# Routed experts, latent attention and the feed-forward's end: another order of the steps on four engines

## The reference

```python
x = x + grouped_attention(layernorm(x), ctx, ctx)            # 32 query heads, 8 key heads
x = x + routed_ffn(layernorm(x), ...)                        # 8 experts + 4 "zero" ones, best 2
x = x + latent_attention(layernorm(x), ctx, Wq, w_kc_q, ...) # 16 heads, rotary, latent of 192 and 64
x = x + mx_ffn(layernorm(x), w_gate, w_up, w_down)           # block-quantised feed-forward
# routed_ffn: w[b,s,e] = 1.5 * prob for the best two of 12
#   out = sum_e w_e * down_e(silu(gate_e(y)) * up_e(y)) + y * sum of the weights of the zero experts
# mx_ffn: inputs and weights in blocks of 32 with a shared power of two, elements rounded and clipped
```

## Time and profile before

| | us |
|---|---|
| median of 3 runs | 820.71 (819.5 to 823.96) |
| profiled execution, its own time | 820.66 |
| its span, first to last instruction | 818.8 |
| PE busy in the span | 751.6 (92%) |
| DVE busy | 597.1 (73%) |
| POOL busy | 567.7 (69%) |
| ACT busy | 404.4 (49%) |

### The profile page before, as it was taken

One profiled execution on the slowest core, in us unless ns is written; L12 is line 12 of the kernel. 1 busy time (PEld: TensorE's weight loads), 2 busy tenths in 40 slices (PEclk: granted clock), 3 DMA queues, 4 the chain that ended last, 5 costly groups with the idle time before them and its releaser, 6 DMA issues. The chain is left out here.

```text
span 818.8 us, 14824 instructions
## 1 busy us (share of the span) xinstructions
PE 751.6 (92%) x4808; PEld 539.1 (66%) x4808; DVE 597.1 (73%) x1087; ACT 404.4 (49%) x1068; POOL 567.7 (69%) x590
## 2 busy tenths in 40 slices
PE   4999999878999998889999999999999999876786
PEld 2555455457888887756777777777777777663454
DVE  5899999866777878666465575886678676739995
ACT  1688888532323323226455545545454545444463
POOL 5667766434867667365666878787878787817996
PEclk9999999999999999899999999999999999987999
DMA  9200000040100010321200000000000000000001
GB/s 252 119 1 0 0 0 1 1 171 1 39 20 19 19 58 0 107 82 63 87 12 1 1 1 2 2 1 1 1 1 2 2 1 1 1 2 7 26 29 44
DMA packets 8764, 24.12 MB, mean 29 GB/s; under 512 B 1712, under 2 KB 5168, under 8 KB 8088
## 3 DMA queue, kind: packets, MB, share of 16 engines
q1 hardware_dynamic: 8154, 23.28, 8.6%
q10 hardware_dynamic: 549, 0.08, 0.1%
HBM read 21.26 MB, written 2.10 MB: 29 GB/s over the span
## 5 line engine op out<-in xcount | busy, mean ns | idle before, releaser
L1620 POOL TENSOR_TENSOR q<-turned 64x512 f32<-64x512 f32 x128 | 167.9, 1312 | 25.5 <-DVE turned L1546 9.9
L1297 PE MATMUL ps<-l_yt,a 128*128 128x512 f32 x576 | 145.5, 403 | 2.1 <-ACT p L1443 1.6
L1297 PEld LDWEIGHTS ps<-l_yt,a 128*128 128x128 f32 x576 | 105.8, 190 | 27.7 <-issue 4.7
L1607 POOL TENSOR_TENSOR p<-p,l_inverse 128x512 f32<-128x512 f32 x64 | 66.9, 1047 | 76.4 <-DVE l_inverse L1568 75.9
L1443 ACT ACTIVATE p<-ps,l_negmax 128x128 f32<-128x128 f32 x256 | 91.0, 382 | 43.2 <-DVE l_negmax L1537 43.1
L1546 DVE TENSOR_TENSOR turned<-ps,rope 128x1024 f32<-128x1024 f32 x64 | 78.1, 1221 | 44.4 <-PE ps L1297 41.7
L879 PE MATMUL ps<-yt_experts,wsplit 128*128 (+1 forms) x384 | 97.2, 402 | 0.2 <-DVE inner L977 0.2
L467 DVE TENSOR_REDUCE negmax<-ps 128x4 f32<-128x512 f32 x128 | 84.3, 685 | 12.8 <-PE ps L290 12.2
L879 PEld LDWEIGHTS ps<-yt_experts,wsplit 128*128 128x128 f32 x384 | 71.2, 192 | 14.4 <-DVE inner L977 0.5
L1537 DVE TENSOR_REDUCE l_negmax<-ps 128x4 f32<-128x512 f32 x64 | 41.2, 686 | 45.9 <-PE ps L1355 45.7
L383 ACT ACTIVATE pt<-ps 128x512 f32<-128x512 f32 x128 | 70.9, 599 | 6.1 <-PE ps L312 3.8
(11 more groups left out here) (214 smaller groups left out, 1549.6 us busy)
## 6 DMA issues: line engine op xcount, KB each, us to landing
wide<-in_wide SPq DMA_DIRECT2D x8, 768.0 KB, 4.3
mx_raw<-in_mx SPq DMA_DIRECT2D x8, 384.0 KB, 3.1
x<-in_x SPq DMA_DIRECT2D x4, 512.0 KB, 8.7
ctx_t<-in_ctx_t SPq DMA_DIRECT2D x1, 2048.0 KB, 8.5
out<-x SPq DMA_DIRECT2D x16, 128.0 KB, 1.7
narrow<-in_narrow SPq DMA_DIRECT2D x8, 192.0 KB, 2.6
ktraw<-in_ctx_rows SPq DMA_DIRECT2D x1, 1248.0 KB
wraw<-in_gate SPq DMA_DIRECT2D x1, 1024.0 KB, 18.6
```

The source lines that it names most:

```text
L1297: out = pe.matmul(tile_bank(n, k), a[i][:, pa, kin, k * 128:(k + 1) * 128], yt[j % 2][:, py, kin, :, :].rearrange("p b s -> p (b s)"), sta ...
L1607: pool.tensor_tensor(p[:, head, :, :], p[:, head, :, :], spread(inverse[:, head, :], 2, S), ALU.mult).then_inc(normed[head], 1)
L1620: t = pool.tensor_tensor(out[rows[(head + half) % 2], head, :], turned[rows[head], half, :], turned[rows[head], 2 + half, :], ALU.add)
```

## The change

Experts: on DVE the five instructions of `shift` are cut in two, `shift_up` (three) and `shift_down` (two). In odd steps `hidden` stands between them (in group 0 ahead of the quantising in every step). On POOL x is scaled in x = 5 and 6 instead of 6 and 7, and `ht` of unit 0 is made one step earlier. The last units are written out by hand on each engine (`last`), with a second PSUM bank for the last weights and the last chunk's transposes. The constant `lowest` is set as a 22nd step of the routes.

Latent attention: PE's order is `tile` (3), `narrow_product`, `context` of n-3, `score` of n-1, `turn_p` (both), `project` of n-3 (both); the 128-column matmul of `narrow_product` becomes two of 64 columns. PSUM banks are handed out anew (`ctx_ps`, `turned_p_bank`) with waits that fit; the places of `spare` are handed out anew; the front's parts on DVE move from the end of the step to behind the maxima, some a step later. Feed-forward: scaling back of sequence 14 and of the second half of sequence 15 moves from POOL to DVE.

```diff
@@ experts, PE: the end written out
+                pe.wait_ge(h_made, UNITS - 2)
+                spread_weights(UNITS - 2, weight_ps)
+                pe.wait_ge(gated_made, UNITS - 1)
+                spread_weights(UNITS - 1, last_weight_ps)
+                down(UNITS - 3)
+                pe.wait_ge(inner_made, UNITS - 1)
+                turn_tiles(CHUNKS - 2)
+                down(UNITS - 2)
+                down(UNITS - 1)
+                pe.wait_ge(mx_kept, CHUNKS - 1)
+                turn_tiles(CHUNKS - 1)
@@ experts, DVE step
-                if first and u == 2:
+                early = first and u < EXPERTS
+                if inside(u - 2, UNITS) and early:
                     hidden(u, par)
                 if inside(v, UNITS):
-                    (shift if x % 2 else block_powers)(v, jv, xv)
+                    if x % 2:
+                        shift_up(v, jv, xv)
+                    else:
+                        block_powers(v, jv, xv)
...
-                if inside(u - 2, UNITS) and not (first and u == 2):
+                if inside(u - 2, UNITS) and not early:
                     hidden(u, par)
+                if inside(v, UNITS) and x % 2:
+                    shift_down(v, jv, xv)
@@ experts, POOL step
-                if inside(u, UNITS) and x == 7:
+                if inside(u, UNITS) and x == 6:
                     pool.wait_ge(affine, j + 4)
+                if first and u == 2:
+                    low_part(0, 0)
+                if inside(u - 3, UNITS) and not (first and u == 3):
+                    low_part(u - 3, old)
                 if inside(v, UNITS):
+                    quantise(4 * jv + xv // 2, xv)
                 if inside(u, UNITS) and x < ROTARY_STEPS:
                     rotate_context(pool, m, rotated, j, x)
-                if inside(u, UNITS) and x in (6, 7):
+                if inside(u, UNITS) and x in (5, 6):
                     scale_x(j, x)
@@ latent attention, PE
-                    pe.matmul(q_ps, b[i][:, 1, :], q[n % 2][:, 2, :], start=False, stop=True).then_inc(narrowed, 1)
+                    for head in range(2):
+                        t = pe.matmul(q_ps[rows[head], :], b[i][:, 1, head * CE:(head + 1) * CE], q[n % 2][:, 2, :],
+                                      start=False, stop=True)
+                    t.then_inc(narrowed, 1)
...
                 narrow_product(n - 1)
                 spare(n, 1)
+                context(n - 3)
+                score(n - 1)
                 turn_p(n - 2, 0)
+                turn_p(n - 2, 1)
+                spare(n, 2)
                 project(n - 3, 0)
-                turn_p(n - 2, 1)
                 project(n - 3, 1)
-                spare(n, 2)
-                score(n - 1)
-                context(n - 2)
                 spare(n, 3)
@@ latent attention, DVE
                 maximum(n - 2, 1)
+                for k, part in ((3, f.add), (4, f.statistics), (6, f.scales), (7, f.divide), (8, f.clip), (9, f.multiply)):
+                    if front_in(n, k) is not None:
+                        part(dve, m, front_in(n, k))
                 rotate_both(n, 0)
...
-                for k, part in ((2, f.add), (3, f.statistics), (6, f.scales), (7, f.divide), (8, f.clip), (8, f.multiply)):
-                    if front_in(n, k) is not None:
-                        part(dve, m, front_in(n, k))
@@ feed-forward, DVE at n == B
                 if n == B:
+                    scale_back(n - 2)
                     clip_halves()
+                    scale_back_half()
```

More of the change, by code:

```diff
@@ L821, in routed_experts, with steps @@
         weights_turned_ps = weight_ps[0:WROWS, :]
-        def steps(engine, step):
+        def steps(engine, step, last):
             def group(j):
@@ L831, in steps @@
                 group(j)
-            for x in range(3):
-                step(UNITS + x, GROUPS, x)
+            last()
         @block.sync
@@ L919, in _, with last, spread_weights, down @@
             t.then_inc(logits_turned, 1)
-            steps(pe, step)
+            def last():
+                def spread_weights(u, bank):
+                    pe.matmul(bank, select[:, u % EXPERTS, :], weights_t[:, GROUPS - 1, :],
+                              start=True, stop=True).then_inc(weight_spread, 1)
+                def down(u):
+                    expert = u % EXPERTS
+                    pe.wait_ge(h_lo, u + 1)
+                    for q, (ph, pw) in enumerate(PRODUCTS):
+                        for s in range(4):
+                            t = pe.matmul(down_ps[:, s, :], ht[u % 2][:, ph, s * S:(s + 1) * S],
+                                          w_at(pw, 4 * FFN + expert * E, E), start=False,
+                                          stop=(expert == EXPERTS - 1 and q == 2 and s % 2 == 1))
+                    t.then_inc(down_made, 1)
+                def turn_tiles(c):
+                    pe.wait_ge(mx_made, c + 1)
+                    for i in range(3):
+                        t = pe.transpose(last_mx_ps[:, i * 128:(i + 1) * 128],
+                                         quantised[c % 2][:, i * 128:(i + 1) * 128], m.ident16[:, :])
+                    t.then_inc(mx_turned, 1)
+                pe.wait_ge(h_made, UNITS - 2)
[9 more added lines that the diff above has]
+                turn_tiles(CHUNKS - 1)
+            steps(pe, step, last)
         @block.scalar
@@ L1050, in _ @@
             then(dve.tensor_reduce(r.total[:, :], r.e[:, :, EXPERTS:], AX.X, ALU.add))
+            then(dve.memset(lowest, -6.0))
             assert count[0] == ROUTE_STEPS
-            dve.memset(lowest, -6.0).then_inc(bounded, 1)
-            dve.wait_ge(bounded, 1)
-            steps(dve, step)
+            steps(dve, step, last)
         @block.gpsimd
@@ L1105, in _, with last @@
+            def last():
+                low_part(UNITS - 3, 1)
+                low_part(UNITS - 2, 0)
+                low_part(UNITS - 1, 1)
+                quantise(UNITS // 2 - 1, EXPERTS - 2)
+                quantise(UNITS // 2 - 1, EXPERTS - 1)
+            steps(pool, step, last)
             pool.wait_ge(stats_made, B - 4)
@@ L1202, in _ @@
                 wait(sp, c_made, i - 1)
+                wait(sp, a_made, 2 * (i - 1))
                 load_wide(sp, m, d, i)
@@ L1274, in spare @@
                         pe.wait_ge(y_lo, 2 * j + 1)
-                    turn(j, place, w_ps)
-                if fj is not None and place == 0:
+                    turn(j, place // 2, w_ps)
+                if fj is not None and place == 2:
                     pe.wait_ge(y_lo, 2 * min(fj + 2, GROUPS - 1) + 2)
```

184 lines of the change are left out of this document (116 added, 68 removed).

## The result

The changed kernel takes 834.12 us in the median of its runs (832.3 to 834.94), beside 820.36 for the kernel before on the same chip (819.5 to 823.96): a ratio of 1.0165, with a 95% interval of 1.0144 to 1.0185. It is slower by 13.8 us. Forecast were 828.9, so 8.2, with a range of 815 to 838.

The account below looks back on a forecast made before the run. PE was taken to bound experts and latent stage, DVE the last 86 us. 820.7 + 14.0 (experts) - 7.1 (latent) - 0.4 (feed-forward's end) + 1.7 (clock) = 828.9 us, range 815 to 838.

Parts of the forecast that it names:

- the loop of the experts: Experts, groups 1 to 3: in odd steps PE waits for POOL's late ht, +3.0 a group, +9.1 us in all.
- e: POOL's other work between mx_quantised and ht in odd steps: 0.74, 1.30, 1.89 and 0 us; ht's lateness is e - 0.2.
- group 0: Experts' first group: hidden ahead of all five shift steps makes ht later in odd steps; +4.9 us.
- the end of the experts: Written-out last units: costed at 0, PE having little left to hide them; bounds -1.5 to +1.5 us.
- the latent stage: Latent attention on PE: fewer array shape switches, less some added waits; -7.1 us, bounds -11 to +1.
- The term of the plain step: Steady latent steps: switches of the array's shape saved on PE, 0.34 us by 28 steps, -9.5 us.
- `scales` in its short form: Latent front on DVE: L1647's 1.29 us falls to about 0.19 once POOL is idle; otherwise +5 us.
- the feed-forward's end: Last chain over DVE, POOL and PE's transposes: scaling back moved to DVE gives -0.4 us, -1.0 to +0.6.
- the clock: PE, after new stalls of about 1.8 and 3.6 us: one fall to half clock, +1.7 us, bounds 0 to +8.
- POOL's idle time takes the delay: Rival, experts: 808 us, chance 0.13; decided by quantising ending before s + 2.6 (s: start of PE's spread).
- The latent gain: Rival that it is eaten: score waits, scales stays long or shape switches still cost; 836 us, chance 0.12.
- the clock falls at each stall over 1.7: Rival, PE's clock: +8 us in place of +1.7, giving 835 us; chance 0.08.

Follow-up runs that it names:

- e_work_first: Changed kernel with POOL's rotation or scaling of x put ahead of mx_quantised in odd steps: 814.58 us, ratio 0.9924 to the kernel before.
- e_x_late: Changed kernel with x scaled at x = 6 and 7 again: 832.71 us, ratio 1.0171 to the kernel before.
- e_whole_shift: Changed kernel with shift_down ahead of hidden again in groups 1 to 3: 817.78 us, ratio 1.0001 to the kernel before.
- e_end: Changed kernel with the last chunk's division ahead of the last unit's low part on POOL in the written-out end: 827.55 us.
- l_one_matmul: Changed kernel with the second narrow product as one matmul of 128 columns again, in the new order: 841.26 us.
- l_two_matmuls: Kernel before with the second narrow product as two matmuls of 64 columns, old order: 820.73 us, ratio 1.0006.
- best: Changed kernel with POOL's work ahead of mx_quantised, hidden between the shift parts in group 0, and the last division earlier: 809.08 us, ratio 0.988.

## Why the prediction was right or wrong

**Right, mechanism and size: the loop of the experts.** For groups 1 to 3 the sum was +9.1; the loop's stretch shows +10.0. The stalls forecast at 0.65, 1.5 and 1.8 us in x = 1, 3 and 5 are waits of 0.55, 1.5 and 1.68 in each group. They make the steps behind them 0.8 longer than before (5.37 against 4.56), 0.6 (6.33 against 5.74, which held the 0.92 of before) and 1.95 (6.51 against 4.56), 3.35 a group where the forecast was 3.0; x = 7 has none. e_work_first, e_x_late and e_whole_shift each show that the stall is e's and DVE's order behind the spread.

**Right: group 0, +4.9.** The stalls forecast at 2.0, 3.6 and 1.7 for `ht` of units 1, 3 and 5 measured 1.62, 3.31 and 1.35, and the 1.62 for unit 0 went. Less the 0.80 of before that is +3.9, and the stretch without the clock grew by some 4.1. (For unit 1 the sum took e = 0.74; the work that stood there is the step of x = 3, of 1.27.)

**Wrong: the end of the experts, put at 0 with bounds of 1.5.** It cost 4.5, some 2.0 of it without the clock. The step that failed is "in the last steps PE has little left to hide them": I weighed only PE's work, and not that the stage ends with POOL. The reading of PE's stalls had already left out the longest wait for `ht` of the kernel before, the one of 2.1 us in the end. The list written by hand puts the last division behind the last `ht`; that stood in the change to be read, and in e_end, without it, PE reaches the last chunk 1.75 earlier.

**Right sign, mis-sized: the latent stage, -7.1.** From its first product to step 31 it gained 8.3, in the drain some 0.9 (the feed-forward's steady steps come 14.81 later than before, step 31 15.68), and its first steps carry some 1.1 more half clock; without that it gained some 10.3, near the end of the bounds. The term of the plain step was 0.34 and is 0.45 in most (0.27 in those of 10.60): the 0.05 that I took off for the score's end is not there, since the score takes 1.09 in place of 1.13, and `turn_p` and `project` undivided save another 0.04. The steps with turning and normalising, put at +0.4 each, lose 0.3 in the three turnings against the plain step and 0.1 in three others; one step loses 0.6. The cover of 0.1 before `score` held: ACT makes qs at 626.04 to 626.64, the score starts at 626.79, and PE waits for it in no steady step; 0.15 lie between the two.

```profile
626.04 0.60 ACT L1567 ACTIVATE qs<-ps 128x512 f32<-128x512 f32 x1 [2.23 <-PE ps L1415]
```

That changes of the array's shape cost is shown by l_one_matmul and l_two_matmuls together: the same edit is worth 0.35 a step where it removes a pair of changes, and 0.05 where it moves one. The Trainium skill ("TensorEngine Tiling (Array Packing)", Key Properties) says that a change of the tiling mode drains TensorE, without a price. The trace agrees and gives one: 0.10 more between the two products, 1.01 in place of 0.91. That the further 0.05 to 0.20 a product behind a change are weights that nothing covers is my reading and not shown.

**Right: `scales` in its short form.** The instruction that took 1289 ns in the earlier trace rows takes 183:

```profile
L1754 DVE TENSOR_SCALAR f_yscale<-f_yscale 128x32 f32<-128x32 f32 x3 | 0.5, 183 | 0.1
```

It runs at 536.56 after POOL's last instruction ended at 535.98; in the kernel before it ran at 521.20 amid a row of POOL instructions from 518.51 to 523.78, began and ended within 0.05 us of one of them, and so did the other two. That agrees with the rule on the shared ports (the Trainium skill, "SBUF — State Buffer", Who interferes with whom) that the prediction weighed. No run here holds everything else fixed, so the ports as the cause are argued, not shown.

**Right: the feed-forward's end, -0.4.** Its last matmul comes 14.35 later than before while its steady steps come 14.81 later: -0.46. DVE's added part took 1.85 for sequence 14, between the bounds of 1.2 and 2.1, and 1.03 for the half, and ended 4.3 after the clip, 812.6 on the old scale.

**Mis-sized: the clock, +1.7 with bounds of 0 to 8.** Some 7.6 us of the profiled difference are half clock, most of it in group 0 and around the end of the experts, in or behind stalls of 1.6 to 3.3. The mechanism was named; one fall was priced, and the stretches hold the worth of four or five. The border that the prediction drew between 1.62 and 1.94 isn't there: the 1.62 of the earlier trace rows was followed by half clock too (0.67 in 188 to 192, and its twelve matmuls took 2.93 us), the same stall of 1.61 in l_two_matmuls was not (1.70), nor were the nine of up to 1.68 in the changed loop (1.00). Beside the forecast, the clock adds 5.9, the experts' end 2.0, the loop 0.9 and the time before the experts 1.3, where no code differs (0.2 to 1.4 in the other traces); the latent stage takes 3.2 back and group 0 0.8. That these errors offset each other in part is luck: they leave 6 us in the profiled executions and 5.2 in the medians.

**The rivals.** Whether POOL's idle time takes the delay was to be decided by whether the quantising ends before s + 2.6; it ended at s + 3.1 (294.23 + 0.84 against 291.93), and the stalls came. With POOL's order changed, the same idle time did take the delay; `best`, with two more edits, comes near that rival's 808. The latent gain was not eaten. The rival by which the clock falls at each stall over 1.7 gave 835, close to the result, but not for its reason: stalls of 1.62 lost the clock too, and in e_whole_shift one of 3.34 didn't.

## What to carry to other kernels

An in-order engine that will wait should do what is ready first: the same 1.89 us cost 1.95 a group behind the waiting instruction and 0.15 ahead of it (steps of 6.51 and 4.71 beside 4.56). Before a step is put behind one that waits for another engine, follow each queue to the last of its readers, to the stage's end too, and ask there which engine finishes last. On TensorE, put products of the same array shape next to each other; here one switch moved to another place saved 0.05 us a step, and a pair of switches removed 0.35.

## What the runs showed of the hardware

Two stalls of PE of 3.31 and 3.34 us, at the same place of the same code, were followed by half clock in the next 4 us and by none. In the first the clock fell before the stall was over (0.90 in its window), in the second it did not fall (1.00). In e_whole_shift the time goes with the mean granted clock from 814.7 to 822.2 us, so a difference of some 5 us between two profiled executions can be clock alone. The Trainium skill ("TensorE: Matmul & The Clock Gate", Part 1: The HAM clock gate) says that the point at which the clock changes differs from run to run of one kernel, and that the ramp at the start costs under 1% of a typical span. The first agrees with these runs. The second speaks of the start alone; the spread of these runs, 7.5 us of 818, is of that size, but here it is as large as most edits. What decides between the two outcomes of one stall stays open.
